# The output's linear map folded into the second MLP of a Swin kernel, its products moved to the head of a strip

## What is computed

```python
x2  = relu(x)
sub = depthwise 9x9 conv of x2 with f_ana            # 9 maps per channel
x3  = concat([sub, x2]), channels last               # (8, 56, 56, 160)
for i in (0, 1):                                     # two Swin blocks, windows of 7x7
    a  = LN(x3) ; windows (shifted by 3 in block 1)
    x3 = x3 + proj(attention(a))                     # 5 heads of 32, bias, mask in block 1
    h  = LN(x3)
    x3 = x3 + gelu(h @ w1 + b1) @ w2 + b2            # 160 -> 640 -> 160
x3 = x3 @ linw + linb                                # the output's linear map, 160 -> 144
y  = 9x9 conv of x3 with f_syn, summed over the 9 maps
out = 1x1 conv of concat([y, x3]) + convb            # 16 channels
```

## Time and profile before

| | us |
|---|---|
| median of 3 runs (3506.59 to 3515.65) | 3507.45 |
| the profiled execution | 3515.31 |
| its span | 3513.8 |
| TensorE busy in the span | 3304.6 (94%) |
| VectorE busy | 2322.7 (66%) |
| ScalarE busy | 1936.7 (55%) |
| GpSimd busy | 829.6 (24%) |

### The profile page before, as it was taken

The page is one execution under the profiler, slowest core; times in us unless marked ns, Lnnn a source line. Parts: engine busy times, 40 slices in busy tenths (PEclk is TensorE's granted clock), DMA queues, the critical chain, the costliest instruction groups (busy, mean ns, idle before and its releaser), DMA issues. The chain is left out here.

```text
span 3513.8 us, 95573 instructions
## 1 busy us (share of the span) xinstructions
PE 3304.6 (94%) x35820; PEld 2956.9 (84%) x35820; DVE 2322.7 (66%) x6840; ACT 1936.7 (55%) x4582; POOL 829.6 (24%) x1625
## 2 busy tenths in 40 slices
PE   7995999999999999999999999999999999999679
PEld 6883888888888888888888888888888888888579
DVE  1114677777777777777777777777777777777332
ACT  1112566666666666666666666666666666666221
POOL 5300222222222222222222222222222222222100
PEclk9996999999999999999999999999999999999789
DMA  5321111111111111111111111111111111111275
GB/s 110 85 73 46 30 35 34 34 33 30 33 34 34 34 34 34 34 34 39 48 27 36 35 35 29 35 24 35 35 35 29 34 24 35 35 35 23 47 137 92
DMA packets 246488, 148.38 MB, mean 42 GB/s; under 512 B 31430, under 2 KB 245881, under 8 KB 246399
## 3 DMA queue, kind: packets, MB, share of 16 engines
q1 hardware_dynamic: 244694, 147.01, 18.6%
q0 software_dynamic: 1728, 0.48, 0.1%
HBM read 96.80 MB, written 52.50 MB: 42 GB/s over the span
## 5 line engine op out<-in xcount | busy, mean ns | idle before, releaser
L1359 PE MATMUL rm<-w,ht 128*112 128x160 f32 x4480 | 693.7, 304 | 0.0
L1359 PEld LDWEIGHTS rm<-w,ht 128*112 128x112 f32 x4480 | 608.9, 177 | 28.5 <-ACT ht L951 12.9
L951 ACT ACTIVATE ht<-rm 128x448 f32<-128x448 f32 (+1 forms) x640 | 318.7, 498 | 186.8 <-PE rm L111 181.9
L865 POOL TENSOR_TENSOR rs<-ln_tmp,mhalf 112x4 f32<-112x4 f32 (+1 forms) x128 | 125.5, 981 | 1047.9 <-DVE ln_tmp L1034 1047.9
L933 ACT ACTIVATE ot_hi<-ra 128x98 fp32r<-128x98 f32 x512 | 103.1, 257 | 455.9 <-PE ra L1338 455.9
L896 ACT ACTIVATE qm<-ra,qmask 128x392 f32<-128x392 f32 x512 | 258.6, 588 | 12.1 <-PE ra L111 3.4
L1149 DVE TENSOR_TENSOR xo<-rm,x1b 112x160 f32<-112x160 f32 (+1 forms) x384 | 134.3, 350 | 190.7 <-PE rm L1359 186.8
L111 PE MATMUL rm<-z2t_hi,w_hi 128*128 128x448 f32 (+1 forms) x640 | 250.7, 392 | 3.0 <-DVE z2t_rest L1139 1.1
L1307 PE MATMUL s_ps<-kt,qm 128*49 128x49 f32 x8192 | 241.2, 211 | 0.9 <-DVE sc L1094 0.9
L1307 PEld LDWEIGHTS s_ps<-kt,qm 128*49 128x49 f32 x8192 | 209.1, 126 | 36.4 <-issue 30.8
L111 PE MATMUL rm<-z2t_rest,w_rest 98*128 98x448 f32 (+1 forms) x640 | 219.9, 344 | 0.0
(11 more groups left out here) (216 smaller groups left out, 9541.7 us busy)
## 6 DMA issues: line engine op xcount, KB each, us to landing
xa<-xs SPq DMA_DIRECT2D x128, 245.0 KB
xr<-xs SPq DMA_DIRECT2D x128, 245.0 KB
xs<-a_tok SPq DMA_DIRECT2D x8, 1960.0 KB, 9.4
xs<-xo SPq DMA_DIRECT2D x64, 245.0 KB
ys<-yz SPq DMA_DIRECT2D x64, 245.0 KB
c_y<-ys SPq DMA_DIRECT2D x48, 260.0 KB
c_y<-ys SPq DMA_DIRECT2D x16, 280.0 KB
c_taps<-in_f_syn SPq DMA_DIRECT2D x24, 126.0 KB, 4.9
```

The lines of the kernel that those rows point to most:

```text
L865: gp.tensor_tensor(rs[1][:, t0:t0 + nt], ln_tmp[1][5][:, t0:t0 + nt], mhalf[:, 0:nt], ALU.pow).then_inc(s_pow, 1)
L951: act_(ht[:, f * SN + t0 * TT:f * SN + (t0 + nt) * TT], bank_m(i, lm, use)[:, 0:nt * TT], ACT.Gelu_apprx_tanh).then_inc(m_freed(i, lm, use ...
L1359: last = mm(bank_m(i, lm, use)[0:TT, t * DIM:(t + 1) * DIM], ht[:, c:c + TT], keep.w["w2", lm][:, f * DIM:(f + 1) * DIM], start=(f == 0), ...
```

## The change

1. lin is applied to the parts of the sum. With z the second layer norm's output before its gain, x1 = z * std + mean, so x1 @ lin = std * (z @ lin) + mean * (column sums of lin). The products L0 to L3 read z2t as `mlp_in` does, and T3 with its splits and repeats goes.
2. W2 of block 1 is replaced by W2 @ lin, b2 by b2 @ lin plus the linear and output bias. This is done at the end of phase A: 10 transposes of W2, 20 fp32 products, 6 for bias and column sums, with ScalarE turning the transposes out and VectorE the results.
3. TensorE runs L0 to L3 between `mlp_in` and `mlp_out(0)`. The ring's order becomes G, L, W, T2.
4. VectorE evicts L with `linear_out`: one scalar_tensor_tensor a tile, yz = L * std + x1b. `mlp_out` then adds W to yz. std is a reciprocal of rs at the head of VectorE's body. ScalarE's copies to yz go.
5. For block 1 x1b is mean * column sums + b2, two operations of GpSimd over all seven tiles.
6. yz is stored once W5 is evicted. xo has no repeated channels any more.
7. In the setup, b2 of block 1 comes in two small loads as a column, and convb as rows.

The core of the diff:

```diff
+            act.wait_ge(s_w2T, 1)
+            nc.scalar.activation(w2t_a[:, 0:4 * 128], nat_ps[:, 0:4 * 128], ACT.Copy)
+            nc.scalar.activation(w2t_a[:, 4 * 128:MLP], mir_ps[:, 0:128], ACT.Copy)
+            nc.scalar.activation(w2t_c[0:REST, 4 * 128:MLP], mir_ps[0:REST, 128:256], ACT.Copy)
+            nc.scalar.activation(w2t_c[0:REST, 0:4 * 128], psum[2][0:REST, 0:4 * 128], ACT.Copy).then_inc(s_w2t, 1)
             act.wait_ge(s_brow, 1)
...
+            nc.vector.tensor_copy(lin_a[:], psum[6][:, 0:DIM])
+            nc.vector.tensor_copy(lin_c[:], psum[6][0:REST, DIM:2 * DIM]).then_inc(s_lin, 1)
...
+            dve.wait_ge(s_fold, 1)
+            for f0, nf, o in FOLD:
+                nc.vector.tensor_copy(keep.w["w2", 1][:, f0 * DIM:(f0 + nf) * DIM], o[:, 0:nf * DIM])
+            nc.vector.tensor_copy(keep.lin_sum[:], psum[7][0:TT, DIM:2 * DIM])
+            nc.vector.tensor_copy(keep.w["b2", 1][:, 0:K * C], psum[7][0:TT, 0:K * C])
+            nc.vector.tensor_tensor(keep.w["b2", 1][:, K * C:DIM], psum[7][0:TT, K * C:DIM], convb_row[:], ALU.add)
...
+            pe.wait_ge(s_brow, 1)
+            w2_1 = keep.w["w2", 1]
+            for f in range(FT):
+                oa = nat_ps[:, f * 128:(f + 1) * 128] if f < 4 else mir_ps[:, 0:128]
+                oc = psum[2][0:REST, f * 128:(f + 1) * 128] if f < 4 else mir_ps[0:REST, 128:256]
+                nc.tensor.transpose(oa, w2_1[:, f * DIM:f * DIM + 128], keep.ident[:])
+                last = nc.tensor.transpose(oc, w2_1[:, f * DIM + 128:(f + 1) * DIM], keep.ident[:])
+            last.then_inc(s_w2T, 1)
+            pe.wait_ge(s_lin, 1)
+            pe.wait_ge(s_prep, 1)
...
+            pe.wait_ge(s_w2t, 1)
+            for f0, nf, o in FOLD:
+                for f in range(f0, f0 + nf):
+                    cols = slice((f - f0) * DIM, (f - f0 + 1) * DIM)
+                    nc.tensor.matmul(o[:, cols], w2t_a[:, f * 128:(f + 1) * 128], lin_a[:], start=True, stop=False)
+                    last = nc.tensor.matmul(o[:, cols], w2t_c[0:REST, f * 128:(f + 1) * 128], lin_c[:], start=False, stop=True)
+            last.then_inc(s_fold, 1)
...
-        RM = [Ring(MLP_USES + T2, 2, {}), Ring(MLP_USES + LIN_USES + T2, 2, {})]
+        RM = [Ring(G_USES + W_USES + T2, 2, {}), Ring(G_USES + LIN_USES + W_USES + T2, 2, {})]
...
+                        gp.tensor_tensor(view(x1b, 0, TT, 0, tiles), view(keep.lin_sum, 0, TT, 0, [[0, ST], [1, DIM]]),
+                                         view(mean[1], 0, TT, 0, [[1, ST], [0, DIM]]), ALU.mult).then_inc(s_xm, 1)
+                        pool.wait_ge(s_xm, i - NS + 1)
+                        ins = gp.tensor_tensor(view(x1b, 0, TT, 0, tiles), view(x1b, 0, TT, 0, tiles),
+                                               view(keep.w["b2", 1], 0, TT, 0, [[0, ST], [1, DIM]]), ALU.add)
...
+                def linear_out(n):
+                    use = f"L{n}"
+                    t0, nt = LPAIRS[n]
+                    dve.wait_ge(*m_full(i, 1, use))
                     if n == 0:
                         dve.wait_ge(s_x1b, m + 1)
+                        reach(dve, s_yz, 64 * (m - NS))
+                        dve.wait_ge(s_std, m - NS + 1)
+                    for t in range(nt):
+                        cols = slice((t0 + t) * DIM, (t0 + t + 1) * DIM)
+                        ins = v.scalar_tensor_tensor(yz[:, cols], bank_m(i, 1, use)[0:TT, t * DIM:(t + 1) * DIM],
+                                                     std[:, t0 + t:t0 + t + 1], x1b[:, cols], ALU.mult, ALU.add)
+                    ins.then_inc(m_freed(i, 1, use)[0], 1)
...
+                if lm == 1:
+                    dve.wait_ge(s_pow, 2 * m + 2)
+                    reach(dve, *m_linear_freed(i))
+                    v.reciprocal(std[:], rs[1][:]).then_inc(s_std, 1)
                 if ln is not None:
                     dve.wait_ge(s_xa, 32 * (i + 2))
                     stats(0, xa, i + 1)
...
                     normalise(0, z1, xa, i + 1, [(0, ST)])
+                if lm == 1:
+                    for n in range(4):
+                        linear_out(n)
                 if lm is not None:
                     mlp_out(0)
...
                     mlp_in(range(2 * FT))
+                if lm == 1:
+                    linear(range(4))
+                if lm is not None:
                     mlp_out(0)
```

More of the change, by code:

```diff
@@ L145, in __init__ @@
             self.w["b2", l] = sb(f"b2_{l}", [TT, DIM])
-        self.w["lin", 1] = self.split(sb, "lin", DIM)
+        self.lin = self.split(sb, "lin", DIM)
+        self.lin_sum = sb("lin_sum", [TT, DIM])
     @staticmethod
@@ L164, in phase_a @@
         nat_ps, mir_ps, conv_ps = psum[0], psum[1], psum[3:]
-        taps = [sb(f"a_taps{n}", [TT, NJ * TT]) for n in range(2)]
+        taps = [sb(f"a_taps{n}", [128, MLP]) for n in range(2)]
         band_hi = sb("a_band_hi", [TT, K * NJ * TT], F32R)
@@ L185, in phase_a @@
             starts[m[:2]], width = width, width + m[2]
-        starts["lin", 1], width = width, width + DIM
         brow = sb("brow", [CK, width])
@@ L488, in _ @@
             dve.wait_ge(s_pool, 2)
-            hi, lo, rest = keep.w["lin", 1]
+            hi, lo, rest = keep.lin
+            nc.vector.tensor_copy(lin_a[:], psum[6][:, 0:DIM])
+            nc.vector.tensor_copy(lin_c[:], psum[6][0:REST, DIM:2 * DIM]).then_inc(s_lin, 1)
             nc.vector.tensor_copy(hi[:], psum[6][:, 0:DIM])
@@ L494, in _ @@
                                     rest[2 * REST:CR, :].bitcast(F32), ALU.subtract)
-            for m, l, banks in (("qkv", 0, (0,)), ("w1", 0, (1, 2)), ("qkv", 1, (3,)), ("w1", 1, (4, 5)), ("lin", 1, (7,))):
+            for m, l, banks in (("qkv", 0, (0,)), ("w1", 0, (1, 2)), ("qkv", 1, (3,)), ("w1", 1, (4, 5))):
                 c0 = starts[m, l]
-                left = {"qkv": 3 * DIM, "w1": MLP, "lin": DIM}[m]
+                left = {"qkv": 3 * DIM, "w1": MLP}[m]
                 for b in banks:
@@ L868, in body @@
                         repeat_rest(z2, s_z[1], *HALF[hf])
-                    for t in range(ST):
-                        ins = gp.tensor_tensor(x1b[:, t * DIM:(t + 1) * DIM], x1[:, t * DIM:(t + 1) * DIM],
-                                               keep.w["b2", la][:], ALU.add)
+                    if la == 0:
+                        for t in range(ST):
+                            ins = gp.tensor_tensor(x1b[:, t * DIM:(t + 1) * DIM], x1[:, t * DIM:(t + 1) * DIM],
+                                                   keep.w["b2", la][:], ALU.add)
+                    else:
+                        tiles = [[DIM, ST], [1, DIM]]
+                        gp.tensor_tensor(view(x1b, 0, TT, 0, tiles), view(keep.lin_sum, 0, TT, 0, [[0, ST], [1, DIM]]),
[3 more added lines that the diff above has]
+                                               view(keep.w["b2", 1], 0, TT, 0, [[0, ST], [1, DIM]]), ALU.add)
                     ins.then_inc(s_x1b, 1)
@@ L1003, in body @@
                 if la is not None:
-                    t_hi("T2", 1)
+                    t_hi(1)
             bodies(act, body)
@@ L1371, in projection, with linear @@
                     filled_a(use, last)
+                def linear(ns):
+                    for n in ns:
+                        use = f"L{n}"
+                        t0, nt = LPAIRS[n]
+                        room_m(use)
+                        for t in range(nt):
+                            c = slice((t0 + t) * TT, (t0 + t + 1) * TT)
+                            o = bank_m(i, 1, use)[0:TT, t * DIM:(t + 1) * DIM]
+                            last = split_passes(nc, o, z2t[0][:, c], z2t[1][:, c], z2t[2][0:CR, c],
+                                                keep.lin[0][:], keep.lin[1][:], keep.lin[2][0:CR, :], False)
+                        filled_m(use, last)
                 def mlp_turned(z, name, hf):
@@ L1437, in body @@
                     scores(0, i + 1)
-                if lm == 1:
-                    pe.wait_ge(*m_freed(i, 1, "T3C1"))
-                    for n, (t0, nt) in enumerate(LPAIRS):
-                        use = f"L{n}"
-                        room_m(use)
-                        for t in range(nt):
-                            c = slice((t0 + t) * TT, (t0 + t + 1) * TT)
-                            last = split_passes(nc, bank_m(i, lm, use)[0:TT, t * DIM:(t + 1) * DIM], *[z[:, c] for z in z2t],
-                                                *[w[:] for w in keep.w["lin", 1]], False)
-                        filled_m(use, last)
                 if ln is not None:
```

113 lines of the change are left out of this document (56 added, 57 removed).

## The result

The changed kernel takes 3523.91 us (median of 8 runs, 3520.47 to 3527.70) where the kernel before takes 3511.10 beside it (8 runs, 3504.22 to 3516.36). The ratio is 1.0037, with a 95% interval of 1.0026 to 1.0048: slower by 9 to 17 us. The forecast was +24.6 us and 3532, with 3506 to 3547 as its range: the sign and the strip loop came as forecast, but the ten products of W2 with the map were charged as twenty.

A forecast was written before the change was run, and what follows sets the result against it. TensorE, busy 94% of the span, was taken as the bound. Strips +12.6, fold +17.4, small load +0.5 and ends -5.9 gave +24.6 us on the median 3507.45: 3532.0 us, range 3506 to 3547.

The forecast's parts named there:

- the strip loop: Block-1 strips: 48.34 us each against 47.92, +0.42 a strip, +12.6 us over 30 strips.
- the block-0 strip is a measured model of the strip that the change leaves: Strip loop: a block-1 strip without T3 and without L at its old place takes block 0's 44.60 us.
- The head block: Block-1 strip head, L0 to W0: L products and waits for evictions cost 3.74 us, against 2.87 in the tail.
- the reader of a finished tile starts 0.29 us after the next tile's first product: Head block: L1 starts at 2387.49, so VectorE can take L0 at 2387.78, 0.29 us later.
- Rival C: Head evictions: VectorE slower, a pair takes 0.98 us; loop +31, sum +43, 3550.5 us; chance 0.12.
- Rival D: Head block: waits among the L products vanish, block 2.87 us; -0.45 a strip, 3506 us in all; chance 0.08.
- Rival F: Strip loop: a lead won at the head shrinks tail waits; at 1.5 us a strip, 3487 us; chance 0.12.
- The fold: End of phase A: transposes of W2, 6 and 20 fp32 products, and evictions lengthen the setup by 17.4 us.
- The clock of the fold: End of phase A: fold products run at a granted 0.50, 1.2 GHz, 0.78 us for each fp32 product.
- Rival B: Setup: the fold runs at 2.4 GHz, 0.28 us a product; setup +3.3, sum +10.5, 3518 us; chance 0.18.
- The small load of SP: Setup: about one more small DMA issue ahead of the third image's load, +0.5 us.
- The ends: Last two bodies: -1.3 us from earlier T2, -5.15 from the earlier store, 0.5 allowed for clock; together -5.9.

The follow-up runs named there:

- the split kernel: Against the changed kernel: L0 to L2 at the head, evicted before the normalisation, L3 between W5 and P0; 3489.68 us, ratio 0.9961 to the kernel before.
- the early fold: Against the split kernel: the whole fold moved ahead of and between the bias products; 3475.87 us, ratio 0.9915 to the kernel before.
- the next kernel: Against the early fold: one VectorE operation evicts each of L0 to L2, GpSimd adds x1b; 3474.05 us, ratio 0.9907 to the kernel before.
- the unused buffer: Kernel before plus one unused buffer of 112 x 160 numbers, shifting later buffers by 640 bytes; profiled execution with a span of 3498.3 us.

## Why the prediction came out as it did

**The bound and the model, right.** The step "the block-0 strip is a measured model of the strip that the change leaves" is the strongest one: 44.60 measured with L taken out, to the hundredth.

**The head block, right in size, off in one detail.** 3.74 forecast, 3.77 measured; +0.42 a strip, +0.45 measured. The inner step "the reader of a finished tile starts 0.29 us after the next tile's first product" was taken from a ScalarE row. VectorE starts 1.24 us after L0's first product even when it has stood idle for 3.94 us (the split kernel), not 1.14. The late normalisation, which ended at 2449.52, hid this. The pair of evictions costs 0.74 from its start to L2, where 0.73 was taken. The nearness of 3.77 to 3.74 is in part luck: L2 starts 1.99 after L0 where 1.87 was forecast, and W0 1.78 after L2 where again 1.87 was, because VectorE's first instruction on L2 comes 1.05 after L2's first product and not 1.14. The two errors cancel. Rival C (pair at 0.98) falls: GpSimd's repeat of z1 does run beside the evictions (2449.61, for 0.94 us), and the pair still costs 0.74. Rival D (no waits) falls with the waits of 0.18 and 0.38. Rival F asked for a lead that shrinks the tail waits; P0 still waits 0.30, and strip less block is 44.60, as in block 0.

**The fold, wrong in its count.** The working says "20 products for W2 times lin (15.6)". The loop has five slices with two products each, ten in all. Two records in the profile make one fp32 product; I had that right in the price (0.78 us for one product, 0.83 measured in the fold) and multiplied by twice the number. With ten, the same working gives 17.4 - 7.8 = 9.6 (10.1 with the 0.83), and the runs show +9.9 to +11.0 at equal clock. This term alone takes the sum from +24.6 to +16.8.

**The clock of the fold, right for this kernel, from one of two cases.** The fold ran at a granted 0.50 in the kernel after. I argued from the first execution of the kernel before as if its 0.50 belonged to the products; the second execution shows the same products at 1.00. Idle time did not bring the clock down in the kernel after either: it fell within the last map product (285.38), ahead of the 4.75 us of idle time, and it stayed at 0.50 through the 15.2 us of products without a break from 290.88 to 306.12. In six of the thirteen profiled executions it fell while TensorE was busy with these fp32 products, in three of them 2 us into the stretch. What decides it is not shown. Rival B's condition, a fold at 2.4 GHz, is met in the one profiled execution of the early fold, where TensorE has nothing to wait for between the convolution and the fold's last product; the next kernel, with the same program there, lost the clock within the fold. Rival B's price did not hold either: 0.28 us a product was taken from the W products, and the fold's took 0.47 at a granted 1.00. The Trainium skill, "TensorE: Matmul & The Clock Gate", section "What's actually happening", has activity release the clock and idle time bring it down. The early fold agrees with the first half of that; the kernel after and the first execution of the kernel before do not, since the clock fell in both while TensorE was busy without a break.

**The small load of SP, not to be seen.** Its +0.5 is lost in a scatter of 3.7 us in the same place.

**The ends, right together.** In the last body but one T2 starts 40.9 us after the body's first G product (3262.67 to 3303.57) where it was 42.6 (3241.17 to 3283.74), -1.7 where -1.3 was forecast. From there to the first of the last stores of ys it is 28.7 instead of 33.2 us, -4.6 where -5.15 + 0.5 was forecast; against the second execution of the kernel before, whose stretch is 32.2, it is only -3.5, so that the agreement is not finer than 1 us.

**What no step held.** The last phase's -2.8, which the unused buffer alone brings as well (-2.6). With it and the right count the sum is 12.6 + 9.6 + 0.5 - 5.9 - 2.8 = +14.0; +12.8 was measured between the medians. The total of 3532.0 came within 8.1 us of the measured 3523.91 although the difference was off by 11.8: the kernel before stood 3.65 us higher beside the kernel after than the three runs that the forecast was added to, which is luck.

**Why the change as such loses.** It takes work from TensorE, 14 transposes a strip, which is worth 0.45 us (3.32 - 2.87) and not their 1.4: waits of the tail, such as the 0.30 before P0, stand where they filled the time. It gives back 0.90 us of waits a strip, because a tile pair's way to VectorE and back is longer than the one pair that covers it in two banks, and 10 to 11 us of a serial fold. Neither belongs to the idea: evicting ahead of the normalisation, one tile moved into a standing wait, and the fold moved ahead of and between the bias products give a kernel 0.85% faster than before.

## What to carry to other kernels

When products move to another place, price the round trip of a bank (last product, eviction, next product) against the work that lies between on the other banks; what is missing there is a wait per round, and it is cut by starting the evicting engine's work first, by fewer operations in the eviction, and by taking one tile to a place where the tensor engine waits anyway. Count the instructions of an unrolled loop from the loop, not from the records. Before a term rests on a granted clock in a setup phase, profile the same kernel twice, and compare stretches at the same clock only.

## What the runs showed of the chip that I had not expected

- The granted clock of one and the same stretch of unbroken fp32 products is 1.00 in one execution and 0.55 in the other, 8.6 us in a 3.5 ms kernel.
- A shift of later buffers by 640 bytes a partition, with no other edit, takes 2.6 us off a phase of 192 us (189.3, in one execution, against 191.9 and 192.0), nearly all of it in the first 46 us.
- From a tile pair's first product to VectorE's first instruction on it are 1.24 us at L0, for eight products that need 0.85, and 1.05 at L2, with VectorE idle both times.
- A single GpSimd operation over 1120 columns took 2.06 us with a product and 2.57 with a sum, where 2.7 had been worked out from narrower ones. Beside two GpSimd additions VectorE's normalisation takes 2.98 us in place of 1.99.
- An fp32 product of 160 columns starts 0.83 us after the last at a granted 0.50 and 0.47 at 1.00 in the fold, where the W products of a strip take 0.28.
